# A step of an attention loop on one core: the query projection moved ahead of the probability transposes, the last two transposes moved behind three score tiles

## What is computed

```python
q = hidden_states @ Wq + bq; k = hidden_states @ Wk + bk; v = hidden_states @ Wv + bv
q = _rope(q, pos); k = _rope(k, pos)
scores = jnp.einsum('bgrsd,bgtd->bgrst', qg, k) / jnp.sqrt(jnp.float32(D))
scores = jnp.where(causal, scores, finfo.min)
probs = jax.nn.softmax(scores, axis=-1)
ctx = jnp.einsum('bgrst,bgtd->bgrsd', probs, v)
return ctx @ Wo + bo
```

## Time and profile before

| | |
|---|---|
| median of 3 runs | 845.27 us (844.85 to 846.61) |
| profiled execution, first to last instruction (span) | 844.5 us |
| TensorE matmul busy | 812.5 us, 96% of the span |
| VectorE, ScalarE, GpSimd busy | 584.2 (69%), 514.6 (61%), 344.2 (41%) us |
| granted TensorE clock, mean over the span | 0.996 of full |
| DMA | mean 34 GB/s |

### The profile page before, as it was taken

One profiled execution on the slowest core, in us unless ns is written; L12 is line 12 of the kernel. 1 busy time (PEld: TensorE's weight loads), 2 busy tenths in 40 slices (PEclk: granted clock), 3 DMA queues, 4 the chain that ended last, 5 costly groups with the idle time before them and its releaser, 6 DMA issues.

```text
span 844.5 us, 14449 instructions
## 1 busy us (share of the span) xinstructions
PE 812.5 (96%) x4361; PEld 695.8 (82%) x4361; DVE 584.2 (69%) x1547; ACT 514.6 (61%) x1254; POOL 344.2 (41%) x311
## 2 busy tenths in 40 slices
PE   7789999999999999999999999999999999999986
PEld 6677888888888888888888888888888888887875
DVE  4776767666776767666776767666776767688657
ACT  5767756666666756666666756666666766664210
POOL 4435643354334533354334533354334533240415
PEclk9999999999999999999999999999999999999999
DMA  9201000020101010010101010020101011000002
GB/s 292 63 1 63 14 26 25 1 64 14 50 0 60 15 36 14 0 62 12 50 0 61 13 37 13 0 62 12 50 0 50 0 41 35 1 15 1 1 0 101
DMA packets 27693, 28.56 MB, mean 34 GB/s; under 512 B 3664, under 2 KB 20224, under 8 KB 27664
## 3 DMA queue, kind: packets, MB, share of 16 engines
q1 hardware_dynamic: 27664, 28.20, 10.5%
HBM read 26.10 MB, written 2.10 MB: 33 GB/s over the span
## 4 chain that ended last, share of the span: by engine, by line
issue 45%; POOL 22%; PE 21%; DVE 9%; ACT 2%; DMA 1%; SPq 1%; POOLq 1%; DVEq 0%; ACTq 0%
POOL rope_rot L612 9%; POOL q_lo L589 4%; POOL wq_lo L589 3%; PE ps_proj L272 3%; PE ps_proj L270 3%; PE ps_proj L271 3%; POOL wo_lo L589 2%; PE ps_tr L1063 2%; DVE prob L850 2%; POOL wkv_lo L589 2%; DVE prob L807 1%; DVE rope_cos L766 1%; PE ps_sc L270 1%; PE ps_out L270 1%; PE ps_out L272 1%
## 5 line engine op out<-in xcount | busy, mean ns | idle before, releaser
L807 DVE CUSTOM_DVE_ANT_0 prob<-ps_sc,mask_sb 128x256 f32<-128x256 f32 (+3 forms) x256 | 115.1, 487 | 126.1 <-PE ps_sc L1108 72.3
L483 ACT ACTIVATE prob<-prob,negmax 128x256 f32<-128x256 f32 (+3 forms) x256 | 141.4, 556 | 72.6 <-DVE negmax L807 72.5
L612 POOL TENSOR_TENSOR rope_rot<-rope_rot,sin_sb 128x512 f32<-128x512 f32 x77 | 100.0, 1299 | 195.6 <-ACT rope_rot L420 195.6
L589 POOL TENSOR_TENSOR q_lo<-rope_cos,q_hi 128x512 fp32r<-128x512 f32 x64 | 85.8, 1340 | 193.2 <-ACT q_hi L436 193.2
L418 ACT ACTIVATE rope_rot<-ps_proj,bias_cols 64x512 f32<-64x512 f32 x80 | 54.7, 684 | 127.8 <-PE ps_proj L272 127.4
L850 DVE TENSOR_SCALAR prob<-prob,rinv 128x128 f32<-128x128 f32 (+3 forms) x256 | 117.9, 503 | 4.5
L738 DVE TENSOR_TENSOR pT_lo<-ps_tr,pT_hi 128x384 fp32r<-128x384 f32 (+2 forms) x192 | 100.4, 549 | 8.1 <-ACT pT_hi L459 6.5
L270 PE MATMUL ps_proj<-xT_hi,wq_hi 128*128 128x512 f32 x256 | 105.9, 414 | 0.0
L1063 PE MATMUL ps_tr<-ident,prob 128*128 128x128 f32 x640 | 93.5, 275 | 12.0 <-DVE prob L850 11.5
L738 DVE TENSOR_TENSOR ctx_lo<-ps_ctx,ctx_hi 128x512 fp32r<-128x512 f32 x64 | 44.2, 690 | 83.3 <-ACT ctx_hi L452 83.3
L272 PE MATMUL ps_proj<-xT_hi,wq_lo 128*128 128x512 f32 x256 | 100.8, 394 | 0.0
(11 more groups left out here) (195 smaller groups left out, 1833.4 us busy)
## 6 DMA issues: line engine op xcount, KB each, us to landing
wq_raw<-in_attn_Wq SPq DMA_DIRECT2D x16, 512.0 KB, 4.7
wo_raw<-in_attn_Wo SPq DMA_DIRECT2D x8, 1024.0 KB, 5.4
wk_raw<-in_attn_Wk SPq DMA_DIRECT2D x8, 256.0 KB, 5.2
wv_raw<-in_attn_Wv SPq DMA_DIRECT2D x8, 256.0 KB, 2.7
out<-acc SPq DMA_DIRECT2D x8, 256.0 KB, 2.0
acc<-in_attn_hidden_states SPq DMA_DIRECT2D x4, 256.0 KB, 4.1
acc<-in_attn_hidden_states SPq DMA_DIRECT2D x1, 1024.0 KB, 8.9
wq_raw<-in_ffn_W_base SPq DMA_DIRECT2D x1, 1024.0 KB, 5.4
```

The lines of the kernel that those rows point to most:

```text
L483: return act.activation(prob[:, slot, SCOL[i]:SCOL[i + 1]], prob[:, slot, SCOL[i]:SCOL[i + 1]], ACT.Exp, bias=negmax[:, slot, i:i + 1], sc ...
L589: return pool.tensor_tensor(dst, full, high.bitcast(F32), ALU.subtract)
L612: pool.tensor_tensor(rope_rot[:, slot, :], rope_rot[:, slot, :], sin_sb[:], ALU.mult).then_inc(sin_done, 1)
L807: return nc.vector.tensor_tensor_reduce(out=prob[:, slot, SCOL[i]:SCOL[i + 1]], in0=ps_sc[bank][:, at:at + w], in1=mask_sb[:, S - w:S], sc ...
```

## The change

TensorE begins a step with proj, and transposes afterwards; the first 8 transposes stand between proj and the scores; the last 2 stand behind score tiles 1, 0 and 2. ScalarE's order follows: `rotate` stands ahead of the high parts of the first two batches, and the high part of the third batch stands behind the exponentials of tiles 1, 0 and 2. VectorE, GpSimd and SyncE are not edited. Nothing is added or left out, and no buffer is changed.

```diff
@@ -451,14 +451,6 @@
                         wait(act, wo_done, g * STEPS - (STEPS - TT) if b == 0 else g * STEPS)
                     act.activation(ctx_hi[:, b, h, :], ps_ctx[:], ACT.Copy).then_inc(ctx_hi_d, 1)
 
-                if cur:
-                    N, t = g * STEPS + n, tr_no(g, TR_P[n])
-                    wait(act, pv_done, N)
-                    wait(act, tr_done, t + 1)
-                    act.activation(pT_3[:], ps_tr[(1 + TR_P[n]) % 2][:, 0:P], ACT.Copy)
-                    act.activation(pT_hi[:, PT_T1:PT_T0], ps_tr[(1 + TR_P[n]) % 2][:, P:S], ACT.Copy).then_inc(tr_hi_d, 1)
-                    wait(act, tr_done, t + 2)
-                    act.activation(pT_hi[:, PT_T0:PT_T2], ps_tr[TR_P[n] % 2][:], ACT.Copy).then_inc(tr_hi_d, 1)
                 if isinstance(g, int) and g == 0 and n == 0:
                     q_high(-1, 7)
                     x_high(TT + 2)
@@ -468,14 +460,18 @@
                     m = (n + 2) % STEPS
                     col = g * R + m % R if n < 6 else g * R + (R + m % R)
                     rotate(proj_q(g, n), rope_q(g, n), bank_q(g, n), rope_slot(ROPE_Q[n] + q_shift(g, n)), col)
+                if cur:
+                    N, t = g * STEPS + n, tr_no(g, TR_P[n])
+                    wait(act, pv_done, N)
+                    wait(act, tr_done, t + 1)
+                    act.activation(pT_3[:], ps_tr[(1 + TR_P[n]) % 2][:, 0:P], ACT.Copy)
+                    act.activation(pT_hi[:, PT_T1:PT_T0], ps_tr[(1 + TR_P[n]) % 2][:, P:S], ACT.Copy).then_inc(tr_hi_d, 1)
+                    wait(act, tr_done, t + 2)
+                    act.activation(pT_hi[:, PT_T0:PT_T2], ps_tr[TR_P[n] % 2][:], ACT.Copy).then_inc(tr_hi_d, 1)
                 if first(g) and n == 6:
                     k_high(g, 5)
                 for k in preps(g, n, 0):
                     prep_hi(k)
-                if cur:
-                    wait(act, tr_done, t + 3)
-                    act.activation(pT_hi[:, PT_T2:PT_END], ps_tr[(1 + TR_P[n]) % 2][:, 0:256], ACT.Copy).then_inc(tr_hi_d, 1)
-
                 has_s = cur if n < 7 else nxt
                 slot = (n + 1) % 2
 
@@ -490,6 +486,10 @@
                     exps(0)
                     wait(act, max_done, V0 + 2)
                     exps(2).then_inc(exp_done, 1)
+                if cur:
+                    wait(act, tr_done, t + 3)
+                    act.activation(pT_hi[:, PT_T2:PT_END], ps_tr[(1 + TR_P[n]) % 2][:, 0:256], ACT.Copy).then_inc(tr_hi_d, 1)
+                if has_s:
                     wait(act, max_done, V0 + 3)
                     exps(3).then_inc(exp_done, 1)
                 for k in (*preps(g, n, 1), *preps(g, n, 2)):
@@ -1061,8 +1061,15 @@
 
                     c = SCOL[i] + t * P
                     return nc.tensor.transpose(ps_tr[bank][:, at:at + P], prob[:, slot, c:c + P], ident[:])
+                j = TR_P[n]
+                if cur if n < 6 else nxt:
+                    m = (n + 2) % STEPS
+                    b, h = m // R, m % R
+                    proj_bank_free(g, PROJ_Q[n] + q_shift(g, n), proj_q(g, n))
+                    if b == 0:
+                        wait(pe, wq_lo_d, g * R + (R + h + 1) if n >= 6 else g * R + (h + 1))
+                    project(wq_hi[:, h, :, :], wq_lo[:, h, :, :], b, bank_q(g, n))
                 if cur:
-                    j = TR_P[n]
                     tr_free(g, j)
                     wait(pe, p_ready, g * STEPS + (n + 1))
                     p_tile(3, 3, 0, (1 + j) % 2)
@@ -1074,13 +1081,6 @@
                         last = p_tile(0, i, i * P, j % 2)
                     last.then_inc(tr_done, 1)
 
-                if cur if n < 6 else nxt:
-                    m = (n + 2) % STEPS
-                    b, h = m // R, m % R
-                    proj_bank_free(g, PROJ_Q[n] + q_shift(g, n), proj_q(g, n))
-                    if b == 0:
-                        wait(pe, wq_lo_d, g * R + (R + h + 1) if n >= 6 else g * R + (h + 1))
-                    project(wq_hi[:, h, :, :], wq_lo[:, h, :, :], b, bank_q(g, n))
                 if first(g) and n == 6:
                     x_transpose(TT)
                     x_transpose(TT + 1)
@@ -1089,12 +1089,6 @@
                 early_out = isinstance(g, int) and g == G - 1 and n == 7
                 if early_out:
                     out_heads(g, n, 0, R)
-                if cur:
-                    tr_free(g, j + 2)
-                    for i in range(2, TT):
-                        last = p_tile(2, i, (i - 2) * P, (1 + j) % 2)
-                    last.then_inc(tr_done, 1)
-
                 has_s = cur if n < 7 else nxt
                 m = (n + 1) % STEPS
                 V0 = (g * STEPS + (n + 1)) * SC_PER
@@ -1119,6 +1113,11 @@
                     scores(0, m % 2, 256).then_inc(sc_done, 1)
                     wait(pe, max_done, V0)
                     scores(2, (m + 1) % 2, 0).then_inc(sc_done, 1)
+                if cur:
+                    tr_free(g, j + 2)
+                    for i in range(2, TT):
+                        last = p_tile(2, i, (i - 2) * P, (1 + j) % 2)
+                    last.then_inc(tr_done, 1)
                 for k in preps(g, n, 1):
                     prep(k)
                 late_kv = isinstance(g, int) and g == 0 and n < R
```

## The result

| | before | after |
|---|---|---|
| device time, median | 845.94 us (844.85 to 846.66, 4 runs) | 977.4 us (973.81 to 978.83, 4 runs) |
| ratio | | 1.1545, 95% interval 1.1519 to 1.157 |
| profiled execution: time, span | span 844.5 us | 978.61 us, span 976.8 us |
| a middle group without a fall of the clock | 94.9 us | 109.3 us |

The account below looks back on a forecast made before the run. TensorE was taken as the bound, winning only its waits, with the helpers' written order deciding. Middle groups 82.5 us, group 0 11 and group 7 11 made 104.5 on a span of 844.5: 950 us, range 925 to 974.

Parts of the forecast that it names:

- what bounds: Whole kernel: TensorE, busy 96% of the span, gains only its waits; ScalarE's and VectorE's written order decides, not their load.
- Waits of the transposes: Every step: the last two transposes wait for VectorE's first low part, start near T+5.80, and lose 1.0 us.
- Output heads: Steps 3 and 7: the first output head waits for VectorE's addition of the last block, until T+7.03; +2.2 us.
- Tile 3 on the masking: Steps 1 and 5: query tile 3's score tile waits for VectorE's masking, starting at T+8.84; step 13.49 us, +3.3 us.
- The sum for a middle group: Eight steps of a middle group: 2 x (0.94 + 3.3 + 0.44 + 2.2) = 13.8 us; six groups 82.5.
- the thinnest margin: GpSimd's low parts of K and Q after steps 1 and 5, needed at T+3.6 of the next step; priced within the bounds.
- groups 0 (from step 1 on) and 7: First and last groups: 11 us more in each, group 0's from its steps 1 to 7.
- what it moves: All steps: TensorE's issue time stays; transposed probabilities reach ScalarE and VectorE later, the first low part ending at T+5.75.
- rival 3: Steps 1 and 5: the clock falls in the new pauses in a third to all of 16 steps, +8 to +24 us; chance 0.15.
- the bound for unpriced waits: The 16 steps with K: late steps interlocking worse than followed may add 1 us each, 16 us.
- The other rivals: Whole kernel: output heads don't wait, each step loses only 1.0 us, 894 us, chance 0.06; or no change, chance 0.01.
- rival 1: Every step: the ScalarE and VectorE chain fits behind TensorE, only the gain is left, 832 us; chance 0.03.

Follow-up runs that it names:

- the kernel with the fill: The changed kernel with score tile 2's matmuls computed three times where TensorE waits, 6 more matmuls in each step: 962.04 us, ratio 1.1351.
- the first half alone: The changed kernel with the last two transposes back ahead of the score tiles and their copy ahead of the exponentials: 1056.35 us, ratio 1.2479.
- the version with both links undone: The changed kernel with ScalarE's transpose copies before the query's, VectorE's K rope and addition before its low parts; further reordered, 839.92 us at best.
- the first version with both links undone: The changed kernel with only ScalarE's transpose copies put before the query copies, and VectorE's K rope and addition before the first two low parts: 853.14 us.

## Why the prediction was right or wrong

**Right: what bounds, and where the time goes.** In the middle groups TensorE's order costs nothing by itself; the helpers' written order does. Waits of the transposes: forecast "about 60", 0.8 each as shown, measured 61 of 0.91. Output heads: forecast 30 near 1 us, measured 30, 32.5 us. Tile 3 on the masking: forecast 16, measured 19, 8.3 us. PV and the probabilities were covered, as said. The points on the path of a step fell within 0.11 us of the forecast, its four lengths within 0.2. The sum for a middle group was 13.8 us, measured 14.3 to 14.4; over six groups 3.6 us too little. GpSimd's low parts of K and Q, which I had called the thinnest margin, held.

**Right as far as shown: groups 0 (from step 1 on) and 7, clock apart.** In group 0, step 3 grew by 2.45 (forecast 2.5) and step 4 shrank by 0.61 (0.5). Steps 1 to 7 grew by 17.4 against 11. The 6.4 over it lie in the steps with the clock down: 1, 2, 5 and 7. For steps 5 and 7 the kernel with the fill shows that it was the clock, since it had no fall there and took 1.6 us less in each; for steps 1 and 2, with the rest, no run tells the clock from a wait that was sized wrong. Group 7 grew by 13.2 against 11; with the fill it had no fall and grew by 11.8, so 1.3 were the clock.

**Wrong: the step "what it moves", for group 0's step 0.** The sum has no term for it; it starts with step 1. It grew by 5.7 us. VectorE there has, besides the low parts, two low parts of the input ahead of the masks. Kernel after:

```profile
37.06 1.18 DVE L738 TENSOR_TENSOR pT_lo<-ps_tr,pT_hi 128x384 fp32r<-128x384 f32 x2 [3.76 <-ACT pT_hi L468]
38.16 0.68 DVE L738 TENSOR_TENSOR xT_lo<-ps_ctx,xT_hi 128x512 fp32r<-128x512 f32 x1
38.75 0.68 DVE L738 TENSOR_TENSOR xT_lo<-ps_out,xT_hi 128x512 fp32r<-128x512 f32 x1
39.35 0.41 DVE L807 CUSTOM_DVE_ANT_0 prob<-ps_sc,mask_sb 128x256 f32<-128x256 f32 x1
```

TensorE in the same stretch:

```profile
35.36 0.48 PE L270 MATMUL ps_sc<-k_hi,q_hi 128*128 128x256 f32 x1 [3.53 <-POOL q_lo L589]
...
40.04 0.79 PE L270 MATMUL ps_sc<-k_hi,q_hi 128*128 128x512 f32 x1 [1.68 <-DVE negmax L807]
41.49 0.63 PE L270 MATMUL ps_proj<-xT_hi,wkv_hi 128*128 128x512 f32 x1
```

The tile for query tile 3 starts at 40.04 where it started at 36.99 before: 3.05 us of wait. The other 2.65 are the lower clock, at which these matmuls take 0.63 us in place of 0.39.

Why the clock fell there stands in the first of these rows. In the same step of the kernel before, TensorE waited three times, with the projection between the first wait and the other two:

```profile
29.65 1.25 PE L1063 MATMUL ps_tr<-ident,prob 128*128 128x128 f32 x8 [1.41 <-DVE prob L850]
...
33.87 0.44 PE L1063 MATMUL ps_tr<-ident,prob 128*128 128x128 f32 x2 [0.20 <-DVE pT_lo L738]
35.41 0.39 PE L270 MATMUL ps_sc<-k_hi,q_hi 128*128 128x256 f32 x1 [1.10 <-POOL q_lo L589]
```

The scores start at the same time in both kernels, when GpSimd's low part is there. The projection had filled a part of the time before them; moved ahead, it fills an earlier wait, and what is left is one wait of 3.53 us. The other traces agree. All seven kernels that have the projection first in group 0 and wait there for GpSimd (3.48 to 3.56 us) show a fall within that wait or within 1.3 us behind it, and so does the one with the first half alone (5.83 us, for the first low part). The three whose waits in this step are at most 1.75 us show none, and of the two with a wait of 2.52 us one shows it. So covering one wait made a longer one; the forecast asked only whether the first was covered.

**Wrong: the term for the clock, put at nothing in the sum and left to rival 3 with 0.15.** The forecast let the clock stay up, and its argument was that waits of 1.75 us in group 0 had not made it fall and that two transposes and an output head break the new pauses. The runs speak against it: pauses of 0.95 and 1.44 us, so broken, did bring a fall in step 1 of group 1 (at 168.6 us), though the like ones of group 3, shown above, did not, and the shorter ones of steps 3 and 7 did as well. And step 0 of group 0 had a wait of twice 1.75. A fall of 3.4 us cost 1.6 us, as the 1.5 said. By the steps that had one, the falls cost 2.65 + 6.4 in group 0, 6.4 in group 1, 3.2 in group 4 and 1.3 in group 7, together some 20 us. The kernel with the fill, which still has falls in group 0, bounds this from below: 15.3 us less the 1.6 behind the last group, 13.7. The case that came nearest was rival 3, with its 958 to 974; the measured 977.4 lies above it too.

**The sum closes.** 104.5 as forecast, 3.6 for the middle groups, 3.05 for step 0, 1.1 for group 7 and what lies behind it (0.8 and 0.3), and 20 for the clock are 132.3 us, as between the spans (132.3). It closes in part by construction, since the clock's share in steps 1 and 2 of group 0 is what was left over. The range failed because its upper end took the clock's 24 us as the largest case, with none of the bound for unpriced waits on top of it. Two slips are small beside this: the median was put 0.8 us above its span, where 1.8 is the distance between time and span, and 0.15 us on 62 steps is 9.3 us, not 8.

**The other rivals fell.** The chain did not fit behind TensorE, and the output heads did wait. But rival 1 tells what the version with both links undone does: when the low part comes early enough, little but a gain is left, 839.92 us at best, where the rival had 832.

What is open: why groups 1 and 4 had falls and 2, 3, 5 and 6, with the same code and the same waits, had none. No run here tells that. That VectorE's sum takes 1.41 us because of GpSimd's work beside it was read from rows, and not tried by itself.

## What to carry to other kernels

When a producer's work is moved so that it covers a wait, ask in which order its in-order consumers will now meet it: here 11 us of waiting were won, and ScalarE's two copies of 0.7 us, set ahead of the copies that TensorE needs first, lost 65. Do not move the consumers' instructions along only because the producer's moved: put first, on each helper, what the bounding engine will want first, and follow every instruction that stands between, in the first group as well. Ask too what the moved work had filled where it stood: here it left one wait of 3.5 us. And where a forecast adds some 1 us of pause to each of 60 steps, put a price for the lower clock into the sum rather than into a rival.

## What the runs showed of the hardware

- Work that waits for nothing can be cheaper than a pause: 384 matmuls more made the kernel 15 us faster, since the granted clock stayed at its upper level from group 1 to the last.
- The same looped code with the same waits had four falls in one group and none in the next, and how many there are varies between executions too: the four runs of the change are 973.81 us at a mean granted clock of 0.976, 976.19 at 0.972, and 978.61 and 978.83 at 0.969.
- Most runs of before lie at two levels, near 845.0 at a granted clock of 0.998 and near 846.5 at 0.996. The profiled one has a fall near 806 us and takes 67.1 us behind its last group; the kernel with the fill, the first version with both links undone (853.14 us), and the one with only the last two transposes moved don't have it, and take 65.8.
- VectorE's sum of two operands in SBUF took 0.69 us where GpSimd was idle and 1.41 us beside a GpSimd product of 1.28; the addition before it, with one operand in PSUM, ran into the same product and kept its 0.68. The two with all operands in SBUF did not share the time: one waited for the other. In the kernel before, 77 of the 80 sums met no GpSimd instruction and took 0.68 to 0.69; the three that started beside a running one took 1.66 to 1.67 and ended 0.55 us after it. In the version with the additions first one sum started 0.07 us ahead of GpSimd's product: the sum kept its 0.69, and the product took 1.76 in place of 1.28.
